# Reordering the slot of a Mamba-2 layer with routed experts: B and C first, the next sequence's first chunk before the additions, and a mean square summed in four column groups

## The chip, the cores and the metric

The kernel runs on one core of a Trainium2 chip. The metric is the device time of one execution in microseconds (us), the median of several runs; lower is better. The profile comes from one further execution.

## What is computed

Sixteen sequences of 512 tokens of width 128 go through two layers. The first is a Mamba-2 block: an input projection gives z (256 wide), x (256), B (128), C (128) and one step size for each of 4 heads; x, B and C pass a causal convolution of 4 taps and a SiLU; then a state-space scan runs over the tokens; its result y is normalised, gated and projected back. The second is a mixture of 8 experts of which each token takes 2.

```python
xBC = silu(conv(x @ Win.T) + conv_b)          # x_ssm, B, C
h   = dA_t * h + (dt_t * x_t) B_t             # for each token, head by head
y_t = C_t . h + D * x_t
yn  = y * rsqrt(mean(y * y) + eps) * norm_w   # the mean square of the change
out = (yn * silu(z)) @ Wout.T
x   = layernorm(x + out)
x   = layernorm(x + experts(x))               # top 2 of 8
```

## The kernel before, in words

Each engine has its program written out by hand; semaphores join them. Phase one is a row of slots. In slot s the scan of sequence s runs in four chunks of 128 tokens (c = 0 to 3), while sequence q = s + 1 is projected and convolved and sequence r = s - 1 (and s - 2) is routed, that is its rows are written to DRAM sorted by expert. A preparatory slot (`enter_all`) precedes slot 0; slots 1 to 14 have the same content, slot 15 projects nothing. Phase two takes the sorted rows through the experts, tile by tile, from about 402 us on; the change doesn't touch it.

The scan of a chunk, by engine:

- TensorE (`slot_pe`): `exponents` (L527: six bf16 matmuls, the logarithms of the decays for 4 heads, into bank `pl[c % 2]`), transposes of the chunk's x and B (L715 to L723), the matmul of C with the carried state (L727), one block of the next sequence's projection (`project_block`, L512), the masked products with x (L750, weights of 64 columns), the carried part (L756), and the new state (L767).
- ScalarE (`slot_act`): `exp_exponents` (L847), copies of B and of the first state (L1016, L1010), tap 0 of the convolution (`tap0`, L911), the squares of y (`square`, L976).
- VectorE (`slot_dve`): `mask_chunk` (L1222: decays times the products of B and C, `Gm`), the x scaled by its step (`Xdt`, L1429), `carried` (L1435), taps 1 to 3 (L1141), y (L1449), state (L1455).
- GpSimd (`slot_pool`): the x scaled for the state (`decay_x`, L1709), the decayed state (`decay_state`, L1703), the gate (`gate_y`, L1659), the places of the routed rows (`place_rows`) and eight indirect DMA writes (`scatter`, L1696), strictly in the order written.

Between the last chunk of slot s and the first of slot s + 1 lies the border. TensorE: `z_block(q, 0)` (L520), the column sums of the squares (L781: for each chunk two matmuls with the squares as weights and 96 columns of ones moving), four output blocks (L802), in between the transposes of the next x (`turn_first_x`, L594), then `inner_products` (L658: B times C of the next sequence, into bank p7) and `z_block(q, 1)`. ScalarE: four SiLUs of the convolution in the order x, x, B, C (`activate`, L917), two products with the skip weight (L922), the gate's two SiLUs (L933) with the copy of the products (`keep_products`, L928) between them. VectorE: the last taps, the gates' top two, the mean square from p7 (L1484), the picks, the four additions of the residual (`residual`, L1247), and in the next slot the first mask and the first scaled x. GpSimd: scatters and the power -1/2 (L1762).

ScalarE holds one table of functions at a time; Exp and SiLU lie in different ones, so an `ACT_TABLE_LOAD` stands in its stream where a chunk's first Exp follows the SiLUs, and one where the SiLUs follow. TensorE's projection into bank `pj[0]` for the next slot waits until ScalarE has read z out of that bank:

```python
if k == 0:
    wait(pe, sz_ready, CC * (q.n - 1) + 1)
```

Of the kernel before, what the change touches and what calls it, by code (L numbers as in the profile page):

```python
# [33 lines left out]
XC = CC + 2  # L34
TAPS = 4
# [20 lines left out]
SP_STEPS = 13  # L56
SP_AHEAD = 9
# [35 lines left out]
def build(nc, t, out):  # L93
    ctx = ExitStack()
    with ctx:
# [78 lines left out]
        gt = sb("gt", [P, CC, TOKS])  # L174
        ms = sb("ms", [P, NC])
# [97 lines left out]
        def y_bank(j):  # L273
# [28 lines left out]
                     "sp_step", "a_ready", "tap_done", "conv_done", "carried_ready", "ln_step", "ve_ready", "shift_ready",  # L302
                     "u_ready", "gate_step", "chosen_ready", "ms_ready", "pos_step", "rank_read",
                     "rows_ready", "parts_ready", "split_step")
        (x1_ready, Gm_ready, M_ready, Xdt_ready, v_ready, yv_ready, state_ready, sp_step, a_ready,
         tap_done, conv_done, carried_ready, ln_step, ve_ready, shift_ready, u_ready, gate_step, chosen_ready,
         ms_ready, pos_step, rank_read, rows_ready, parts_ready, split_step) = [sem(n) for n in names_dve]
        names_pool = ("slot_ready", "place_step", "picks_made", "Xdd_ready", "decayed_ready", "g_ready", "rms_ready", "rstd_ready", "scaled_ready")
        (slot_ready, place_step, picks_made, Xdd_ready, decayed_ready, g_ready, rms_ready, rstd_ready, scaled_ready) = [sem(n) for n in names_pool]
        scattered = [[sem(f"scattered_{'AB'[k]}{i}") for k in range(2)] for i in range(2)]  # L310
        table_step = sem("table_step")
# [55 lines left out]
        def out_place(c):  # L367

            return (p5, c * OUTW) if c + 1 < NC else (p4, 0)
# [136 lines left out]
        def _(pe):  # L506
            def project_block(q, k):
                if k == 0:
                    wait(pe, sz_ready, CC * (q.n - 1) + 1)
                else:  # L510
                    wait(pe, conv_done, XC * q.n + k - 1)
                pe.matmul(pj[k % 2][:, :], w_xbc[:, k * P:(k + 1) * P], xT[:, q.n, :],  # L512
                          start=True, stop=True).then_inc(proj_psum, 1)
# [92 lines left out]
            def enter_all():  # L606
# [38 lines left out]
                steps_of(3)  # L645
                turn_steps(3)
# [5 lines left out]
            def inner_products(q):  # L652

                pe.wait_ge(xc_ready, XC * (q.n + 1))
# [42 lines left out]
            def slot_pe(s, scan, project, route):  # L697
# [4 lines left out]
                for c in range(NC):  # L702
                    tok = slice(c * P, (c + 1) * P)
                    n = NC * s.n + c
                    if scan and c != 1 and (c + 1 < NC or project):
                        if not route and c == 0:
                            pe.wait_ge(steps_kept, SEQS // GROUP)
                        exponents(s if c + 1 < NC else q, (c + 1) % NC)
                    if scan:
                        pe.wait_ge(Xdt_ready, n) if not isinstance(n, int) or n > 0 else None  # L710
                        wait(pe, Btok_ready, (NC - 1) * s.n + c)
                        if c == 0:
                            wait(pe, x1_ready, NC * s.n)
                        if c == 0:
# [14 lines left out]
                    if project:  # L729
# [46 lines left out]
                if scan:  # L776
                    pe.wait_ge(sq_done, NC * (s.n + 1))
                    pe.wait_ge(yv_ready, NC * (s.n + 1))
                    for c in range(NC):
                        for k in range(CC):  # L780
                            mm = pe.matmul(p7[:, c * PADN:(c + 1) * PADN], ysq[:, k, c * P:(c + 1) * P],  # L781
                                           ones[:, 0:PADN], start=(k == 0), stop=(k == CC - 1))
                    mm.then_inc(ss_psum, 1)
                if scan:
# [4 lines left out]
                    for c in range(NC):  # L789
                        if c + 1 == NC:  # L790
# [4 lines left out]
                            elif project:  # L795
                                pe.wait_ge(S_ready, q.n + 1)
                                turn_first_x(q)
# [7 lines left out]
                if project:  # L805
                    inner_products(q)
# [29 lines left out]
        def _(act):  # L836
# [71 lines left out]
            def tap0(q, c):  # L908
                act.wait_ge(proj_psum, XC * q.n + c + 1)
                wait(act, xc_ready, XC * (q.n - 1) + c + 1)  # L910
                act.activation(acc[:, c, :], pj[c % 2][:, :], ACT.Identity, bias=conv_b[:, c:c + 1],  # L911
                               scale=conv_w[:, c, TAPS - 1:TAPS]).then_inc(tap0_done, 1)

            def activate(q, k):
                act.wait_ge(conv_done, XC * q.n + k + 1)
                wait(act, y_psum, NC * (q.n - 1))
                act.activation(xc[q.par][:, k, :], acc[:, k, :], ACT.Silu).then_inc(xc_ready, 1)  # L917

            def skip_part(q, k):
                act.wait_ge(xc_ready, XC * q.n + k + 1)  # L920
# [14 lines left out]
            def enter_all():  # L935
# [26 lines left out]
                keep_steps(3)  # L962
                enter_dt(1, G0, SEQS)
# [887 lines left out]
```

## Time and profile before

| | |
|---|---|
| runs | 701.42, 702.55 and 702.74 us, median 702.55 us |
| profiled execution | 699.86 us, its span on the core 698.0 us |
| TensorE clock granted, mean | 0.977 |
| busy share of the span | TensorE 91%, VectorE 78%, ScalarE 69%, GpSimd 67% |
| one slot in the steady part | 22.5 us |

A row of a timeline gives the start of an instruction (or of several alike), its length, engine, line, operation and tiles, and in brackets how long the engine had been idle and who ended that. Lengths of two neighbours can overlap: an engine starts the next instruction before the last one's result is out. So what an instruction costs its engine is the distance of two starts, and what it costs a waiter is its length. A float32 matmul shows as two records.

### The profile page before, as it was taken

Reading aid. Unit: us, or ns where it says so; the run is one execution under the profiler, and the core shown is the slowest. Engines: PE = TensorE matmul, PEld = TensorE weight load, DVE = VectorE, ACT = ScalarE, POOL = GpSimd, SP = SyncE. Lnnn points to the kernel's source line nnn. Section 1 sums busy time; section 2 is a strip of 40 time slices with the busy share of each in tenths; the row PEclk is TensorE's granted clock in tenths of the full one; section 3 lists DMA queues with packets and bytes.
Section 4 is the critical chain, followed back from the end, with each engine's and each line's share of the span. In section 5 each row is a group of like instructions: output and inputs, shape, how many; then the busy total and the mean of one; then the engine's idle time right before and its main releaser. Section 6 shows DMA issues by size and latency. Waiting matters only on the chain.

```text
span 698.0 us, 19510 instructions
## 1 busy us (share of the span) xinstructions
PE 633.0 (91%) x4811; PEld 507.4 (73%) x4811; DVE 542.1 (78%) x1852; ACT 479.5 (69%) x1210; POOL 466.9 (67%) x696
## 2 busy tenths in 40 slices
PE   6789999999999999999998789999999999999900
PEld 4356666666566766666665589999999999999900
DVE  4688898899988998889989577776666666888844
ACT  5567877887787878887786377556665566677724
POOL 5023287788777887788777857777755555777754
PEclk9999999999999999999999999999999999999965
DMA  9280001110111011110110123323422223455352
GB/s 248 56 301 17 13 24 35 39 48 24 38 36 45 29 38 32 44 47 25 35 36 32 43 60 88 92 76 110 98 75 71 74 73 101 137 183 176 122 201 100
DMA packets 56668, 54.50 MB, mean 78 GB/s; under 512 B 9562, under 2 KB 45918, under 8 KB 56304
## 3 DMA queue, kind: packets, MB, share of 16 engines
q1 hardware_dynamic: 45840, 33.67, 17.5%
q0 software_dynamic: 8416, 16.93, 7.1%
q10 hardware_dynamic: 2304, 2.65, 1.1%
q8 instruction: 44, 0.72, 0.5%
q14 instruction: 64, 0.52, 0.3%
HBM read 31.05 MB, written 22.63 MB: 77 GB/s over the span
## 4 chain that ended last, share of the span: by engine, by line
PE 62%; issue 11%; POOL 9%; ACT 6%; DVE 5%; DMA 4%; SPq 1%; DVEq 1%; POOLq 0%; ACTq 0%
PE p L693 12%; PE pl L684 8%; PE pj L512 5%; PE p L684 4%; PE p L756 3%; PE p L727 3%; PE p L781 3%; PE p L750 3%; POOL moe_rows L1772 3%; PE p L802 3%; PE p L767 3%; PE pj L520 2%; PE p L658 2%; PE pj L676 1%; PE pl L533 1%
## 5 line engine op out<-in xcount | busy, mean ns | idle before, releaser
L1772 POOL DMA_INDIRECT moe_rows<-xT x135 | 135.5, 1004 | 78.9 <-DVE xT L1389 49.0
L1696 POOL DMA_INDIRECT sorted_rows<-pair,slot x128 | 128.6, 1005 | 30.6 <-issue 28.4
L1141 DVE SCALAR_TENSOR_TENSOR acc<-pj,conv_w_sb,acc 128x511 f32<-128x511 f32 (+2 forms) x192 | 141.0, 735 | 8.6 <-ACT acc L911 6.8
L693 PE MATMUL p<-w,xT 128*128 x1080 | 143.7, 276 | 2.2 <-ACT xT L1058 1.7
L1058 ACT ACTIVATE xT<-pl,b_sb 128x128 f32<-128x128 f32 x360 | 102.7, 368 | 48.7 <-PE pl L684 46.2
L693 PEld LDWEIGHTS p<-w,xT 128*128 128x128 f32 x1080 | 131.4, 192 | 3.5 <-issue 3.4
L684 PE MATMUL pl<-xT 128*128 128x128 f32 x720 | 95.1, 275 | 1.6 <-DVE xT L1377 1.6
L684 PEld LDWEIGHTS pl<-xT 128*128 128x128 f32 x720 | 87.5, 192 | 1.8 <-issue 1.8
L1385 DVE TENSOR_TENSOR xT<-p,b_sb 128x128 f32<-128x128 f32 x135 | 39.2, 290 | 63.1 <-PE p L693 58.3
L1058 ACT ACTIVATE xT<-p,b_sb 128x128 f32<-128x128 f32 x180 | 51.4, 370 | 23.9 <-PE p L684 23.7
L512 PE MATMUL pj<-xT,w_xbc 128*128 128x512 f32 x128 | 67.2, 607 | 0.0
L911 ACT ACTIVATE acc<-pj,conv_b_sb,conv_w_sb 128x512 f32<-128x512 f32 x64 | 49.7, 777 | 22.2 <-PE pj L512 21.3
L1709 POOL TENSOR_TENSOR Xdd<-Xdt,cur 128x256 f32<-128x256 f32 x48 | 29.5, 615 | 45.3 <-DVE Xdt L1429 32.0
L1377 DVE COPY xT<-w 128x512 f32 x135 | 58.7, 435 | 0.0
L750 PEld LDWEIGHTS p<-M,Xdt 128*64 128x64 f32 x512 | 26.8, 136 | 43.7 <-issue 42.9
L1659 POOL TENSOR_TENSOR gt<-yv,sz 128x256 f32<-128x256 f32 x64 | 47.1, 735 | 9.5 <-DVE yv L1449 8.8
L1389 DVE SCALAR_TENSOR_TENSOR xT<-xT 128x128 f32<-128x128 f32 x135 | 49.4, 366 | 4.8
L1222 DVE TENSOR_TENSOR M<-pl,Gm 128x512 f32<-128x512 f32 x64 | 43.9, 686 | 11.4 <-issue 8.5
L847 ACT ACTIVATE pl<-pl 128x512 f32<-128x512 f32 x64 | 37.2, 582 | 20.8 <-PE pl L538 20.6
L684 PE MATMUL p<-xT 128*128 128x128 f32 x360 | 47.6, 275 | 0.0
L750 PE MATMUL p<-M,Xdt 128*64 128x128 f32 x512 | 42.1, 285 | 2.0 <-issue 1.2
L684 PEld LDWEIGHTS p<-xT 128*128 128x128 f32 x360 | 43.7, 192 | 0.0
(235 smaller groups left out, 1340.2 us busy)
## 6 DMA issues: line engine op xcount, KB each, us to landing
xT<-sorted_rows SPq DMA_DIRECT2D x135, 65.0 KB
xres<-in_x SPq DMA_DIRECT2D x16, 256.0 KB, 3.1
w<-in_w SPq DMA_DIRECT2D x2, 2048.0 KB, 10.0
acc<-moe_rows SPq DMA_DIRECT2D x12, 256.0 KB, 3.8
xT<-moe_rows SPq DMA_DIRECT2D x12, 256.0 KB, 5.4
out<-sz ACTq DMA_DIRECT2D x10, 256.0 KB, 2.4
moe_rows<-xT POOLq DMA_INDIRECT x135, 2.3
sorted_rows<-pair,slot POOLq DMA_INDIRECT x128
```

Of the source, the lines that this page charges most:

```text
L512: pe.matmul(pj[k % 2][:, :], w_xbc[:, k * P:(k + 1) * P], xT[:, q.n, :], start=True, stop=True).then_inc(proj_psum, 1)
L684: mm = pe.matmul(h_bank[j % 3][:, f * P:(f + 1) * P], w1e[j % 4][:, f * P:(f + 1) * P], sT[j % 4], start=True, stop=True)
L693: mm = pe.matmul(y_bank(j)[:, 0:P], hT[j % 4][:, f, :], w2[:, bass.ds(e, 1), f, :].rearrange("p e d -> p (e d)"), start=(f == 0), stop=(f ...
L750: mm = pe.matmul(p7[half, (h // 2) * P:(h // 2 + 1) * P], Xdt[c % 2][:, h * HD:(h + 1) * HD], M[c % 2][:, h, :], start=(h < 2), stop=(c == ...
L911: act.activation(acc[:, c, :], pj[c % 2][:, :], ACT.Identity, bias=conv_b[:, c:c + 1], scale=conv_w[:, c, TAPS - 1:TAPS]).then_inc(tap0_do ...
L1058: act.activation(hT[j % 4][:, f, :], h_bank[j % 3][:, f * P:(f + 1) * P], ACT.Gelu, bias=b1[:, bass.ds(e * FB + f, 1)]).then_inc(hT_ready, 1)
L1141: ins = dve.scalar_tensor_tensor(out=acc[:, k, j:TOKS], in0=pj[k % 2][:, 0:TOKS - j], scalar=conv_w[:, k, TAPS - 1 - j:TAPS - j], in1=acc[ ...
L1377: dve.tensor_copy(w1e[j % 4], w1[:, bass.ds(expert[j], 1), :].rearrange("p e f -> p (e f)")).then_inc(w1e_ready, 1)
L1389: dve.scalar_tensor_tensor(out=ye[j % 8], in0=ye[j % 8], scalar=xs[k][:, P + 1:P + 2], in1=xs[k][:, 0:P], op0=ALU.mult, op1=ALU.add).then_ ...
L1659: pool.tensor_tensor(gt[:, :, c * P:(c + 1) * P], yv[c % 2][:, :, :], sz[s.par][:, :, c * P:(c + 1) * P], ALU.mult).then_inc(g_ready, 1)
L1696: pool.indirect_dma_start(out=sorted_rows[:, :], out_offset=bass.IndirectOffsetOnAxis(slot[q.par][:, c, k:k + 1], 0), in_=(rowA, rowB)[k][ ...
L1772: pool.indirect_dma_start(out=moe_rows[:, :], out_offset=bass.IndirectOffsetOnAxis(xs[k][:, P:P + 1].bitcast(I32), 0), in_=ye[j % 8], in_o ...
```

## The change

1. The blocks of the projection are taken in the order B, C, x, x (`ORDER`), so B and C are convolved and activated first.
2. `inner_products` needs only B and C and moves between the second and the third output block; `turn_first_x` goes right behind it. ScalarE copies the products before the skip products, and both gate SiLUs come last.
3. From slot 1 on, `mask_chunk(q, 0)` and the scaled x of the next sequence's chunk 0 come before `residual` on VectorE, and its `decay_x` comes ahead of the last scatter on GpSimd.
4. `exponents` of chunk 1 of the next sequence are computed in chunk 3 of this slot, together with those of chunk 0, and both are exponentiated there. At the border no Exp is left; the first one of a slot is that of chunk 2. In the preparatory slot the same is done for sequence 0.
5. `project_block(q, 0)` goes ahead of the transpose of B.
6. The mean square: the ones become the weights (32 columns), the squares move, and chunk c writes partitions 32c to 32c + 31 (its own group of columns of the array). ScalarE copies the 128 x 128 sums (`keep_sums`, behind the first SiLU), TensorE transposes them after the first output block, VectorE reads the mean square from there.

```diff
+ORDER = (*range(CC, XC), *range(CC))
...
         def out_place(c):
-            return (p5, c * OUTW) if c + 1 < NC else (p4, 0)
+            return (p5, (c - 1) * OUTW) if c > 0 else (p4, 0)
...
             def turn_first_x(q):
-                pe.wait_ge(xc_ready, XC * q.n + CC)
+                pe.wait_ge(xc_ready, XC * (q.n + 1))
...
             def inner_products(q):
-                pe.wait_ge(xc_ready, XC * (q.n + 1))
+                pe.wait_ge(xc_ready, XC * q.n + XC - CC)
...
             # enter_all, TensorE
                 steps_of(3)
+                pe.wait_ge(steps_kept, SEQS // GROUP)
+                exponents(q, 1)
                 turn_steps(3)
...
             # slot_pe
-                    if scan and c != 1 and (c + 1 < NC or project):
-                        if not route and c == 0:
-                            pe.wait_ge(steps_kept, SEQS // GROUP)
-                        exponents(s if c + 1 < NC else q, (c + 1) % NC)
+                    if scan and c == 2:
+                        exponents(s, 3)
+                    if project and scan and c == 3:
+                        exponents(q, 0)
+                        exponents(q, 1)
...
                         if c == 0:
+                            if project:
+                                project_block(q, 0)
                             wait(pe, x1_ready, NC * s.n)
...
-                    for c in range(NC):
-                        for k in range(CC):
-                            mm = pe.matmul(p7[:, c * PADN:(c + 1) * PADN], ysq[:, k, c * P:(c + 1) * P],
-                                           ones[:, 0:PADN], start=(k == 0), stop=(k == CC - 1))
+                    for k in range(CC):
+                        for c in range(NC):
+                            mm = pe.matmul(p7[Q * c:Q * (c + 1), 0:P], ones[:, 0:Q], ysq[:, k, c * P:(c + 1) * P],
+                                           start=(k == 0), stop=(k == CC - 1), skip_group_check=True)
...
+                        if c == 1:
+                            pe.wait_ge(sums_kept, s.n + 1)
+                            pe.transpose(p7[:, P:2 * P], kept[:, :], ident[:, :]).then_inc(turned_psum, 1)
+                        if c == 2 and project:
+                            inner_products(q)
+                            if route:
+                                turn_first_x(q)
...
             # slot_act
-                    if scan and (c + 1 < NC or project):
+                    if scan and 0 < c < NC - 1:
                         exp_exponents(n + 1, c + 1)
+                    if scan and project and c == NC - 1:
+                        exp_exponents(n + 1, 0)
...
                     if scan and c > 0:
                         square(s, c - 1)
+                    if scan and project and c == NC - 1:
+                        exp_exponents(n + 2, 1)
...
                     for k in range(XC):
                         activate(q, k)
+                        if k == 0:
+                            keep_sums(s)
+                    keep_products(q)
                     for k in range(CC):
                         skip_part(q, k)
-                    gate_part(q, 0)
-                    keep_products(q)
-                    gate_part(q, 1)
+                    for k in range(CC):
+                        gate_part(q, k)
...
             # slot_dve
-                    dve.wait_ge(ss_psum, s.n + 1)
+                    dve.wait_ge(turned_psum, s.n + 1)
...
+                if project and s.n > 0:
+                    dve.wait_ge(cur_ready, q.n + 1)
+                    mask_chunk(q, 0)
+                    scale_x(q, 0)
                 if scan:
                     residual(s)
...
             # slot_pool
-                    for c in range(2, NC):
-                        scatter(old, c, 1)
+                    scatter(old, 2, 1)
+                if project and s.n > 0:
+                    pool.wait_ge(cur_ready, q.n + 1)
+                    decay_x(q, 0)
+                if scatters:
+                    scatter(old, 3, 1)
```

## Rows read from the trace of the kernel before

**Rows 1.** The page: busy time by engine, and the last chain by engine.

```profile
PE 633.0 (91%) x4811; PEld 507.4 (73%) x4811; DVE 542.1 (78%) x1852; ACT 479.5 (69%) x1210; POOL 466.9 (67%) x696
...
PE 62%; issue 11%; POOL 9%; ACT 6%; DVE 5%; DMA 4%; SPq 1%; DVEq 1%; POOLq 0%; ACTq 0%
```

**Rows 2.** Busy time by window: PE, PEld, DVE, ACT, POOL, granted clock, DMA, GB/s.

```profile
200.00:250.00 50.00, 48.55 (x336) 32.23 (x334) 44.92 (x147) 38.72 (x81) 39.93 (x68) 1.00 0.12 35
```

**Rows 3.** Timeline of ScalarE, one border and the next.

```profile
191.92 0.42 ACT L976 ACTIVATE ysq<-yv 128x256 f32<-128x256 f32 x1 [0.33 <-DVE yv L1449]
192.35 1.28 ACT L917 ACT_TABLE_LOAD   x1
193.65 2.19 ACT L917 ACTIVATE xc<-acc 128x512 f32<-128x512 f32 x4
195.75 1.32 ACT L922 ACTIVATE xD<-xc,skip 128x512 f32<-128x512 f32 x2
196.97 0.57 ACT L933 ACTIVATE sz<-pj 128x512 f32<-128x512 f32 x1
...
198.92 1.28 ACT L847 ACT_TABLE_LOAD   x1
...
200.71 0.27 ACT L1016 COPY Btok<-p 128x128 f32<-128x128 f32 x1
200.87 0.79 ACT L911 ACTIVATE acc<-pj,conv_b_sb,conv_w_sb 128x512 f32<-128x512 f32 x1
...
202.40 0.38 ACT L1010 COPY state<-p 128x256 f32<-128x256 f32 x1
...
214.87 1.28 ACT L917 ACT_TABLE_LOAD   x1
```

**Rows 4.** Timeline of TensorE, the same stretch.

```profile
192.39 2.02 PE L781 MATMUL p<-ones,ysq 128*128 128x96 f32 x16
194.25 1.58 PE L802 MATMUL p<-w_out,gt 128*128 128x136 f32 x12
...
196.35 1.05 PE L658 MATMUL p<-xc 128*128 128x128 f32 x8
197.25 1.02 PE L520 MATMUL p<-xT,w_z 128*128 128x512 f32 x2
...
201.04 0.39 PE L533 MATMUL pl<-too_early,ident_b 128*128 128x512 bf16 x1 [0.34 <-ACT Btok L1016]
...
209.60 0.67 PE L767 MATMUL p<-Xdd,Btok 128*128 128x256 f32 x2
210.11 0.38 PE L533 MATMUL pl<-too_early,ident_b 128*128 128x512 bf16 x1
...
210.76 0.39 PE L721 MATMUL p<-ident,xc 128*128 128x128 f32 x2
211.15 0.70 PE L727 MATMUL p<-state,xc 128*128 128x256 f32 x2
211.69 1.02 PE L512 MATMUL pj<-xT,w_xbc 128*128 128x512 f32 x2
```

**Rows 5.** Timeline of GpSimd, the same stretch.

```profile
193.30 0.75 POOL L1659 TENSOR_TENSOR gt<-yv,sz 128x256 f32<-128x256 f32 x1
...
202.85 0.61 POOL L1703 TENSOR_TENSOR decayed<-state,cur 128x256 f32<-128x256 f32 x1 [0.58 <-ACT state L1010]
...
215.80 0.74 POOL L1659 TENSOR_TENSOR gt<-yv,sz 128x256 f32<-128x256 f32 x1
```

**Rows 6.** Timeline of TensorE and ScalarE at the first slot's border.

```profile
39.21 0.63 PE L538 MATMUL pl<-S,pick_t 96*128 96x128 bf16 x4
...
39.51 1.28 ACT L847 ACT_TABLE_LOAD   x1
```

**Rows 7.** Timeline of ScalarE, first Gelu of phase two.

```profile
405.15 1.28 ACT L1058 ACT_TABLE_LOAD   x1 [8.18 <-PE pl L684]
```

**Rows 8.** Timeline of TensorE, 32-column weights in four groups.

```profile
29.77 1.07 PE L557 MATMUL pl<-xT,w_dt 128*32 128x512 f32 x8
```

More of the change, by code:

```diff
@@ L56 @@
 SP_STEPS = 13
+DT_STEPS = SP_STEPS + 3
 SP_AHEAD = 9
@@ L174, in build @@
         gt = sb("gt", [P, CC, TOKS])
+        kept = sb("kept", [P, P])
         ms = sb("ms", [P, NC])
@@ L310, in build @@
         scattered = [[sem(f"scattered_{'AB'[k]}{i}") for k in range(2)] for i in range(2)]
+        sums_kept = sem("sums_kept")
+        turned_psum = sem("turned_psum")
         table_step = sem("table_step")
@@ L511, in project_block @@
                     wait(pe, conv_done, XC * q.n + k - 1)
-                pe.matmul(pj[k % 2][:, :], w_xbc[:, k * P:(k + 1) * P], xT[:, q.n, :],
+                pe.matmul(pj[k % 2][:, :], w_xbc[:, ORDER[k] * P:(ORDER[k] + 1) * P], xT[:, q.n, :],
                           start=True, stop=True).then_inc(proj_psum, 1)
@@ L728, in slot_pe @@
                                       start=True, stop=True).then_inc(off_psum, 1)
-                    if project:
+                    if project and c > 0:
                         project_block(q, c)
@@ L789, in slot_pe @@
                     for c in range(NC):
-                        if c + 1 == NC:
+                        if c == 0:
                             if not route:
@@ L916, in activate @@
                 wait(act, y_psum, NC * (q.n - 1))
[L917 removed]
+                act.activation(xc[q.par][:, ORDER[k], :], acc[:, k, :], ACT.Silu).then_inc(xc_ready, 1)
             def skip_part(q, k):
[L920 removed]
+                act.wait_ge(xc_ready, XC * q.n + XC - CC + k + 1)
                 wait(act, yv_ready, NC * (q.n - 1))
@@ L962, in enter_all @@
                 keep_steps(3)
+                exp_exponents(1, 1)
                 enter_dt(1, G0, SEQS)
@@ L977, in square, with keep_sums @@
                                ACT.Square).then_inc(sq_done, 1)
+            def keep_sums(s):
+                act.wait_ge(ss_psum, s.n + 1)
+                wait(act, turned_psum, s.n)
+                act.copy(kept[:, :], p7[:, 0:P]).then_inc(sums_kept, 1)
             def normalise(r, k):
@@ L1040, in slot_act @@
                     decay(2, G0, SEQS, 2, 4)
+                if scan and not project:
+                    keep_sums(s)
                 if project:
@@ L1043, in slot_act @@
                         activate(q, k)
+                        if k == 0:
+                            keep_sums(s)
+                    keep_products(q)
                     for k in range(CC):
                         skip_part(q, k)
-                    gate_part(q, 0)
-                    keep_products(q)
-                    gate_part(q, 1)
+                    for k in range(CC):
+                        gate_part(q, k)
             slots(act, slot_act)
@@ L1173, in softplus_step @@
                 else:
-                    dve.wait_ge(sp_step, SP_STEPS * g + k)
+                    dve.wait_ge(dt_step, DT_STEPS * g + k)
                 if k == 0:
@@ L1207, in split @@
                 high, mid, low = (parts[:, lo:hi, Q * k:Q * k + NH] for k in range(3))
-                link = chain(split_step, 3 * g)
+                link = chain(dt_step, DT_STEPS * g + SP_STEPS)
                 dve.wait_ge(sums_psum, g + 1)
@@ L1224, in mask_chunk, with scale_x @@
                                   ALU.mult).then_inc(M_ready, 1)
+            def scale_x(s, c):
+                dve.wait_ge(tr_psum, NC * s.n + c + 1)
+                wait(dve, Xdd_ready, (NC - 1) * s.n + max(c - 1, 0))
+                o, at = x0_bank(s.n) if c == 0 else (p5, 0)
+                dve.tensor_tensor(heads(Xdt[c % 2][:, :]), heads(o[:, at:at + DI]),
+                                  per_head(cur[s.par][:, 0, :], c), ALU.mult).then_inc(Xdt_ready, 1)
             def take_ranks(r):
@@ L1416, in slot_dve @@
                     return
-                if scan:
+                if scan and s.n < 2:
                     dve.wait_ge(cur_ready, s.n + 1)
@@ L1420, in slot_dve @@
                 for c in range(NC):
-                    n = NC * s.n + c
                     if project and c > 0:
                         tap(q, c - 1, 1)
-                    if scan:
-                        dve.wait_ge(tr_psum, n + 1)
-                        wait(dve, Xdd_ready, (NC - 1) * s.n + max(c - 1, 0))
-                        o, at = x0_bank(s.n) if c == 0 else (p5, 0)
-                        dve.tensor_tensor(heads(Xdt[c % 2][:, :]), heads(o[:, at:at + DI]),
-                                          per_head(cur[s.par][:, 0, :], c), ALU.mult).then_inc(Xdt_ready, 1)
+                    if scan and (c > 0 or s.n < 2):
+                        scale_x(s, c)
+                    n = NC * s.n + c
                     if route and c == 0:
@@ L1728, in slot_pool @@
                     return
-                if scan:
+                if scan and s.n < 2:
                     pool.wait_ge(cur_ready, s.n + 1)
```

21 lines of the change are left out of this document (9 added, 12 removed).

## The prediction

> **What bounds the kernel now.** I read the page first: TensorE is busy 91% of the span and carries 62% of the chain that ended last [rows 1]. In 50 us of steady slots it is busy 48.55, VectorE 44.92, ScalarE 38.72, GpSimd 39.93, at full clock [rows 2]. That looks like a kernel bound by TensorE, in which each microsecond saved there counts. A busy share doesn't say that, so I read the timelines of one slot next, and the reader is to see a handing-over in them.
>
> Take as zero the load of the SiLU table at 192.35; the next one is at 214.87, so a slot is 22.52 us [rows 3]. It has two stretches.
>
> *Stretch A, from the SiLU table to the copy of the first state* (192.35 to 202.40 + 0.38 = 202.78): 10.43 us. ScalarE is nearly always at work in it: a table load of 1.30, four SiLUs in 2.10, two skip products in 1.22, gate and products, a second load and the Exp of chunk 1 (198.92 to 200.71, 1.79), the copy of B, tap 0, the Exp of chunk 2, the state. TensorE in the meantime works ahead, then waits for the copy of B (0.34 idle at 201.04) [rows 3, 4].
>
> *Stretch B, from that copy to the next SiLU table*: 12.09 us. Here TensorE goes through chunks 1 to 3 with hardly a gap. GpSimd runs beside it without rest: it begins 0.07 after the copy (202.85) and ends the last gate at 215.80 + 0.74 = 216.54, 13.76 us after the copy [rows 5]. The output blocks need that gate. At the border before, it ended at 193.30 + 0.75 = 194.05, and the output blocks began at 194.25 [rows 4, 5], straight behind the column sums. So TensorE and GpSimd arrive together: a shorter column sum finds the gate not ready.
>
> **The change part by part.** I cost each against these two stretches.
>
> *Column sums.* Eight matmuls take 192.39 to 194.25, 1.86 us [rows 4]. The new form resembles the step sizes' matmul, where four of 512 columns in four groups end after 1.07 [rows 8], while a single one of 512 columns over the full array has a length of 1.02 [rows 4]: the four run side by side. Two rounds at 128 columns should then take some 0.6 (estimate: two quarters of 0.86 and a little for the switch); the upper bound is 1.86, if nothing overlaps. The Trainium skill says the same in "TensorEngine Tiling (Array Packing)", Tiling Modes: up to 4 times faster with 32 columns, but a change of mode drains the array. By its factor alone the sums would take 0.47; the drain is not seen apart in a row here. Saved: about 1.25 of TensorE. Worth on the path: at most the 0.20 between the gate's end and 194.25, and that is eaten by the next item.
>
> *Copy and transpose of the sums.* New: a 128 x 128 copy on ScalarE behind the first SiLU. There is no such row; the copy of B has its shape and holds ScalarE 0.16 (200.71 to 200.87), with its result out after 0.27 [rows 3]. Bounds 0.16 and 0.27. It lies on stretch A, as ScalarE is its bound: +0.16. TensorE stands still for it behind the first output block.
>
> *Border, laid out anew from the load of the SiLU table.* Load 1.30, one SiLU to 1.83, the copy to 1.99 (result 2.10), three more to 3.57. TensorE turns the sums (0.11), ends the second output block at about 2.7 (0.47 each, as three take 1.42 up to 195.67, my estimate from the twelve records), the products take 0.90 (196.35 to 197.25) and their result is out at 3.8. ScalarE so waits 0.23, copies the products (0.48, as the gate's SiLU of the same shape), skip products 1.22 to 5.50, first gate SiLU out at 6.07. Only then may the next projection begin: result 1.02 later, and the transpose of B, now behind it, about 0.15 more: 7.24. Copy of B 0.16, tap 0 0.67, **table load 1.30**, Exp 0.49, state 0.38, with signals: 10.3. Before: 10.43. Gain 0.15 a slot. An Exp has gone from the border, but its table load hasn't: it now stands behind tap 0 and before the Exp of chunk 2, still on the path. Where it stands against that Exp's wait matters. At slot 0's border the load began at 39.51, while the matmuls the Exp waits for ran to 39.84 [rows 6]: it starts ahead of the wait.
>
> *Mask, scaled x, decay_x ahead.* Nothing is added. VectorE gets the products at 4.4, ends mask and scaled x at 5.35 and the four additions at about 6.5; these gate the transpose of B, which is at 7.0 anyway. The cover is the projection in front of it; without that, the 0.9 of the two would show. On GpSimd `decay_x` waits for the scaled x, 5.4, with one scatter queued behind it; both are over by 7.4, and the next thing there needs the statistics at about 8.1. Cost nothing.
>
> *Exponents of chunk 1 moved into chunk 3.* TensorE: six bf16 matmuls, 210.11 to 210.76, 0.65 [rows 4]. Before, they stood at the border, where TensorE has slack; now they stand in stretch B, where it has none. Part is taken back: between 210.76 and 211.15 two transposes and a wait for the state take 0.39, of which I put 0.17 down to the wait, and the restart costs 0.10 (211.15 to 211.69 for 0.44 of work, an estimate). So +0.38. ScalarE gets the Exp (0.49) between two squares; the gap before the last square was 0.33 [rows 3], and it shifts with the rest, so up to +0.05. If rather the whole 0.65 is hidden by the state coming later through VectorE, this is 0; if nothing is taken back, 0.65.
>
> Sum: -0.15 + 0.43 = +0.28 a slot. Laid out with a uniform 0.04 for each signal, where the state's wait is longer, I get +0.08. I take **+0.2**, for 14 steady slots +2.8. Slot 1 has its first x turned behind the projection now, +0.5; the preparatory slot and slot 0 about nothing (turning the steps waits for the new exponents, 0.6, but the products come sooner); slot 15, which projects nothing, starts its scan sooner, -0.5. Phase two is untouched and shifts. Together +2.8, say +3. Against the profiled execution, 699.86 us (span 698.0, 1.9 around it), that is 702.8; against the median of the runs, 2.7 higher, 705.5. I forecast the median.
>
> **The rivals.** What a measurement of this kernel can tell from no change is about 0.2%, 1.4 us.
>
> *Faster: the moved exponents are free.* If stretch B doesn't grow, the slot keeps the 0.15, and up to 0.3 if the border's queue is tighter than laid out: 14 times that, -2 to -4, 699 to 700. In its strong form TensorE itself is the bound, as the chain's 62% says: 1.25 - 0.11 saved 16 times gives -18, 684. Against the strong form: TensorE waits for ScalarE and the gate [rows 4, 5]. It decides from the point where stretch B grows by less than 0.15.
>
> *About the same:* the two stretches cancel, 701 to 704.
>
> *Slower by more: the table load stands behind the wait.* The first Gelu's load began only after 8.18 us of idle time, when its matmul was out [rows 7]. If the Exp of chunk 2 does so, its load starts at 8.7 and not 8.1 in stretch A: +0.55 a slot, 713. The page "ScalarE: Activation LUTs", Step-by-step, of the Trainium skill puts the load right before its ACTIVATE; whether a wait stands between is not said, and [rows 6] speaks for no delay.
>
> *Slower: the groups don't overlap.* Then the sums' copy comes 0.3 later and pushes all SiLUs: +0.3, 709.5.
>
> **How the numbers follow.** Forecast (slower by 1.4 to 6): 0.38. Faster 0.32, of it 0.05 for the strong form. Same 0.20. Table load 0.05, groups 0.05. The predicted time is the likeliest one's, 705.5. The range takes the weak faster form with a margin and the groups' case: 697 to 711, leaving out the strong form, most of the table case and the tails. The likeliest case alone: 704 to 708.5. Faster 0.32, same 0.20, slower 0.48.
>
> **What would show it.** Slot length 22.7 (between two SiLU table loads). Column sums about 0.6, followed by an idle TensorE of some 0.9 until the gate, and another until the copy of the sums. First state copied 10.3 after the SiLU table; TensorE idle about 1.0 ahead of the matmul with the state (L727) in chunk 1. The two exponents side by side in chunk 3, 1.3 long. Tables still 2 a slot. I am wrong if the slot is under 22.4, above all if the border (SiLU table to first state) is under 10 us or stretch B stays at 12.1; or if the residual holds up the transpose of B.

## The result and the profile after

The changed kernel takes 719.95 us (median of 4 runs, 719.07 to 720.29) beside 701.98 us for the kernel before (4 runs, 699.22 to 702.74): ratio 1.0257, 95% interval 1.0228 to 1.0287. The profiled execution took 719.07 us, its span is 717.2 us, 19.2 more than before.

The page, and the busy times of 50 us of steady slots (the lines that answer to [rows 1, 2]):

```profile
PE 625.3 (87%) x4827; PEld 492.5 (69%) x4827; DVE 545.7 (76%) x1852; ACT 479.6 (67%) x1226; POOL 466.0 (65%) x696
...
PE 60%; issue 12%; ACT 11%; POOL 8%; DVE 4%; DMA 2%; DVEq 1%; SPq 1%; ACTq 0%; POOLq 0%
...
L517 PE MATMUL pj<-xT,w_xbc 128*128 128x512 f32 x128 | 68.6, 618 | 8.9 <-ACT sz L947 8.9
```

```profile
200.00:250.00 50.00, 45.52 (x332) 28.55 (x330) 44.14 (x137) 38.16 (x81) 39.12 (x65) 1.00 0.11 36
```

TensorE did 7.7 us less work and the kernel takes 19 us longer. ScalarE's share of the chain has gone from 6% to 11%, and the projection waits for the gate's SiLU, which is new. The slots, each from one SiLU table load to the next, say where the time is (us):

| | before | after | difference |
|---|---|---|---|
| start to the first SiLU load | 33.34 | 33.74 | +0.40 |
| slot 0 | 23.73 | 24.93 | +1.20 |
| slot 1 | 22.52 | 27.00 | +4.48 |
| slot 2 | 22.52 | 23.66 | +1.14 |
| slots 3 to 14 | 12 x 22.55 | 12 x 23.36 | +9.7 |
| last border and slot 15, to the Gelu load | 32.44 | 36.14 | +3.70 |
| phase two | 292.85 | 291.43 | -1.42 |

**A steady slot.** ScalarE's timeline, answering to [rows 3]:

```profile
202.76 1.28 ACT L931 ACT_TABLE_LOAD   x1
204.05 0.63 ACT L931 ACTIVATE xc<-acc 128x512 f32<-128x512 f32 x1
204.59 0.25 ACT L997 COPY kept<-p 128x128 f32<-128x128 f32 x1
204.74 1.67 ACT L931 ACTIVATE xc<-acc 128x512 f32<-128x512 f32 x3
206.73 0.58 ACT L942 COPY Gm<-p 128x512 f32<-128x512 f32 x1 [0.33 <-PE p L665]
207.21 1.33 ACT L936 ACTIVATE xD<-xc,skip 128x512 f32<-128x512 f32 x2
208.45 0.58 ACT L947 ACTIVATE sz<-pj 128x512 f32<-128x512 f32 x1
208.93 0.59 ACT L947 ACTIVATE sz<-p 128x512 f32<-128x512 f32 x1
210.47 0.27 ACT L1038 COPY Btok<-p 128x128 f32<-128x128 f32 x1 [0.95 <-issue]
210.63 0.78 ACT L925 ACTIVATE acc<-pj,conv_b_sb,conv_w_sb 128x512 f32<-128x512 f32 x1
211.43 1.28 ACT L861 ACT_TABLE_LOAD   x1
212.72 0.58 ACT L861 ACTIVATE pl<-pl 128x512 f32<-128x512 f32 x1
213.22 0.38 ACT L1032 COPY state<-p 128x256 f32<-128x256 f32 x1
...
226.12 1.28 ACT L931 ACT_TABLE_LOAD   x1
```

Stretch A, from the load at 202.76 to the end of the state's copy at 213.60, is 10.84 (before 10.43); stretch B is 12.52 (before 12.09). ScalarE now idles twice in A, 0.33 for the products and 0.95 for the transposed B, and the second table load starts only after the second gap. TensorE, answering to [rows 4]:

```profile
202.79 0.65 PE L790 MATMUL p<-ysq,ones 128*32 128x128 f32 x16
204.05 0.73 PE L817 MATMUL p<-w_out,gt 128*128 128x136 f32 x4 [0.61 <-POOL gt L1694]
...
205.57 1.13 PE L665 MATMUL p<-xc 128*128 128x128 f32 x8
...
209.18 1.10 PE L517 MATMUL pj<-xT,w_xbc 128*128 128x512 f32 x2 [0.48 <-ACT sz L947]
210.11 0.27 PE L724 MATMUL p<-ident,xc 128*128 128x128 f32 x1
...
211.48 0.38 PE L543 MATMUL pl<-S,pick_t 96*128 96x128 bf16 x4
...
213.65 0.70 PE L736 MATMUL p<-state,xc 128*128 128x256 f32 x2 [0.97 <-ACT state L1032]
```

The column sums are 0.65 long where they were 2.02. TensorE then waits for GpSimd's last gate (0.61), for the gate's SiLU (0.48) and for the state (0.97).

**The borders that aren't steady.** TensorE's timeline in slot 0, at the border from slot 0 to slot 1, at the last border and in the last slot, and ScalarE's load for the first Gelu:

```profile
39.79 2.08 PE L517 MATMUL pj<-xT,w_xbc 128*128 128x512 f32 x2 [1.97 <-ACT sz L947]
...
58.73 0.64 PE L790 MATMUL p<-ysq,ones 128*32 128x128 f32 x16
61.47 0.98 PE L607 MATMUL p<-vals,ones 128*128 128x192 f32 x2 [2.09 <-DVE parts L1242]
62.24 1.11 PE L817 MATMUL p<-w_out,gt 128*128 128x136 f32 x4
...
394.50 1.13 PE L665 MATMUL p<-xc 128*128 128x128 f32 x8 [1.94 <-DVE ms L1515]
...
395.68 1.83 PE L817 MATMUL p<-w_out,gt 128*128 128x136 f32 x8
...
414.37 0.65 PE L790 MATMUL p<-ysq,ones 128*32 128x128 f32 x16 [0.96 <-ACT ysq L991]
417.28 1.28 PE L817 MATMUL p<-w_out,gt 128*128 128x136 f32 x4 [2.27 <-POOL gt L1694]
418.35 0.42 PE L810 MATMUL p<-ident,kept 128*128 128x128 f32 x1
418.56 2.93 PE L817 MATMUL p<-w_out,gt 128*128 128x136 f32 x12
...
425.77 1.28 ACT L1086 ACT_TABLE_LOAD   x1 [10.43 <-PE pl L691]
```

In the kernel before, the last output blocks were:

```profile
399.93 2.12 PE L802 MATMUL p<-w_out,gt 128*128 128x136 f32 x16 [0.88 <-POOL gt L1659]
```

At 61.47 the sums of the second group of sequences (`sums(G0, SEQS, (ones,), 3)`) wait for a split on VectorE. They share bank p4 with one output block. `out_place` used to give p4 to block 3, now it gives it to block 0, so the wait stands ahead of all four blocks. After the gaps of 2.09 and 2.27 the matmuls take up to twice as long: four records of an output block 1.11 where they take 0.63 at full speed, and in the last slot the twelve records of three blocks 2.93 where they lasted 1.58 [rows 4]. The granted clock of 417 to 426 us is 0.50, the lower of its two levels (1.2 and 2.4 GHz) throughout; that of 60 to 82 us is 0.92, before it was 1.00. At 394.50 the products wait for a mean square that VectorE delivers behind the early part of the routing table. There the eight records of the products are still near full speed, 1.13, and the blocks behind them are not, 1.83 for eight records.

### The profile page after: what moved, and what is told of

Same layout as the page of the kernel before. It is cut to its first block, busy times and chain, and to the rows that moved or that the text cites. A ratio compares the mean times of both kernels' runs of the same rounds, so it can differ in the third digit from the quotient of the medians.

```text
span 717.2 us, 19559 instructions
## 1 busy us (share of the span) xinstructions
PE 625.3 (87%) x4827; PEld 492.5 (69%) x4827; DVE 545.7 (76%) x1852; ACT 479.6 (67%) x1226; POOL 466.0 (65%) x696
## 4 chain that ended last, share of the span: by engine, by line
PE 60%; issue 12%; ACT 11%; POOL 8%; DVE 4%; DMA 2%; DVEq 1%; SPq 1%; ACTq 0%; POOLq 0%
PE p L700 12%; PE pl L691 8%; PE pj L517 8%; PE p L691 4%; PE p L759 4%; POOL moe_rows L1811 3%; PE p L736 3%; PE p L776 3%; PE p L765 3%; ACT xD L936 3%; PE p L665 2%; PE pl L538 2%; PE pl L543 2%; PE pl L540 2%; ACT pl L861 2%
## 5 line engine op out<-in xcount | busy, mean ns | idle before, releaser
L1694 POOL TENSOR_TENSOR gt<-yv,sz 128x256 f32<-128x256 f32 x64 | 47.0, 734 | 10.5 <-DVE yv L1480 9.8
L1250 DVE TENSOR_TENSOR M<-pl,Gm 128x512 f32<-128x512 f32 x64 | 43.8, 684 | 10.5 <-ACT Gm L942 10.2
L817 PE MATMUL p<-w_out,gt 128*128 128x136 f32 x256 | 42.6, 304 | 10.0 <-POOL gt L1694 10.0
L817 PEld LDWEIGHTS p<-w_out,gt 128*128 128x128 f32 x256 | 37.1, 210 | 14.0 <-POOL gt L1694 13.8
```

What stands on the lines that cost most here:

```text
L817: mm = pe.matmul(o[:, at:at + OUTW], gt[:, k, c * P:(c + 1) * P], w_out[:, k, :], start=(k == 0), stop=(k == CC - 1), skip_group_check=True)
```

## The experiments

The kernel before took about 702 us on some devices and about 742 on others. There is no trace of it from the slower ones. Run 1's trace is from one of them: its steady slots are 22.52 as here, and its phase two takes 335.9 where the kernel before took 292.85. So totals are given as ratios to the kernel before on the same device, and slots are compared directly. "Last stretch" is from the last SiLU load to the Gelu load (32.44 in the kernel before).

**1. The column groups alone** (`sums_alone`: the kernel before with part 6).

> The kernel before with part 6 alone (mean square in four column groups, its copy and transpose). Theory of the border: TensorE's saved 1.2 us a slot is not on the path, because the last gate on GpSimd ends only 0.2 us before the output blocks began; the copy of the sums (0.15 on ScalarE) and the wait of the mean square's readers add a little. Slot 22.5 to 22.8, total 702 to 707. Rival 'TensorE is the bound': slot 21.4, total 685. Rival 'the sums' chain is what costs': slot 23.0 or more, total 709 or more.

Ratio 1.0047 (1.0021 to 1.0073). That is inside what was expected. The steady slot stayed 22.52, as TensorE idles 0.96 where it saved 1.2:

```profile
195.04 0.64 PE L785 MATMUL p<-ysq,ones 128*32 128x128 f32 x16
196.65 0.73 PE L809 MATMUL p<-w_out,gt 128*128 128x136 f32 x4 [0.96 <-POOL gt L1675]
...
400.10 0.64 PE L785 MATMUL p<-ysq,ones 128*32 128x128 f32 x16 [0.97 <-DVE yv L1465]
403.01 1.28 PE L809 MATMUL p<-w_out,gt 128*128 128x136 f32 x4 [2.27 <-POOL gt L1675]
...
404.29 2.93 PE L809 MATMUL p<-w_out,gt 128*128 128x136 f32 x12
```

The last stretch grew from 32.44 to 35.59. Before, the longer column sums filled part of the time until the gate and TensorE idled 0.88 there; now it idles 2.27 and comes back at half speed. From the start of these output blocks to the Gelu load it is 8.50 (403.01 to 411.51), before 5.22 (399.93 to 405.15): a saving that is only waited out costs 3.3 in this slot. Slot 0 was 1.0 longer as well.

**2. The exponents alone** (`exps_alone`: the kernel before with part 4).

> The kernel before with part 4 alone (exponents and Exp of the next sequence's chunk 1 in chunk 3, none at the border). Theory: the stretch from the first state's copy to the SiLU table grows by 0.4 as in the changed kernel; the stretch before it loses the Exp (0.49), since in the old order nothing else waits at the border. Slot 22.4 to 22.6, total 700 to 704. Rival 'moving the exponents is the whole loss': slot 22.9 or more, total 708 or more. The load of the Exp table then stands behind tap 0.

Ratio 1.0039 (1.0019 to 1.0059). Slot 22.74: stretch A fell from 10.43 to 9.95, stretch B rose from 12.09 to 12.79. The slot is above the 22.4 to 22.6 that were expected: the move does shorten the border, and the scan gives back more than that.

**3. The changed kernel without part 4** (`exps_back`).

> The changed kernel without part 4: exponents and Exp of chunk 1 back at the border. Theory: the stretch behind the first state's copy falls from 12.52 to 12.1; in the stretch before it the table load moves into the 0.95 us in which ScalarE waited for the transpose of B, so it does not grow although an Exp of 0.49 comes back: 10.84 to 10.3. Slot 22.3 to 22.5, total 704 to 707. Rival 'the border's new order costs, wherever the exponents are': only the 0.4 comes back, slot 22.9 to 23.0, total 713 to 714.

Ratio 1.0137 (1.0108 to 1.0167), steady slot 22.85: A 10.77, B 12.08. Stretch B is the old one again, so its 0.43 belongs to the exponents alone. Stretch A keeps most of its loss, as the rival had it: that loss comes from the orders. At the border of slot 1 this version has the same wait of 2.09 as the changed kernel, but TensorE comes out of it at full speed:

```profile
60.83 0.56 PE L607 MATMUL p<-vals,ones 128*128 128x192 f32 x2 [2.09 <-DVE parts L1240]
61.23 0.63 PE L818 MATMUL p<-w_out,gt 128*128 128x136 f32 x4
```

Its slot 1 takes 24.52, in the changed kernel 27.00.

**4. Output block 0 of sequence 0 in its old place** (`slot0_placed`).

```diff
-        def out_place(c):
+        def out_place(s, c):
+            if s.n == 0:
+                return (p5, c * OUTW) if c + 1 < NC else (p4, 0)
...
-                        if c == 0:
-                            if not route:
+                        if not route and c + 1 == NC:
                                 sums(G0, SEQS, (ones,), 3)
```

> The changed kernel with the output blocks of sequence 0 placed as before (block 3 in bank p4), so that the sums over the late sequences wait for VectorE only ahead of the last block and not ahead of the first. Theory: TensorE's idle 2.1 us and the half clock behind it go; the time from the SiLU table of slot 1's start to the next (27.0 against 22.5 before) falls to about 23.7; total 3 to 4 us less than the changed kernel, 716 to 717. Rival 'VectorE's softplus and the late first x do it': under 1 us less. The steady slot stays at 23.36.

Slot 1 fell from 27.00 to 24.11 and the wait of 2.09 is gone: the place of block 0 is the main cause of slot 1. The ratio, 1.0278 (1.0230 to 1.0325), doesn't show it: the steady slots were 23.52 in this profile, and the last stretch 37.50, both longer than in the changed kernel. In the last stretch the products behind the wait for the mean square ran at half speed here, 2.05 for 1.13. Why stretch B was 12.68 in the steady slots, not 12.52, is not known; the changed kernel was not run on that device.

**5. The changed kernel again** (`after_again`), as the companion of 6 to 8.

> The changed kernel once more, beside the next three, since the last four ran where all kernels take some 40 us longer in phase two. Slower than before by 16 to 20 us, steady slot 23.3 to 23.5.

721.32 us, ratio 1.0262 (1.0223 to 1.0301), slot 23.38.

**6. The first gate's SiLU ahead of the products' copy** (`gate_early`).

```diff
+                    gate_part(q, 0)
                     keep_products(q)
                     for k in range(CC):
                         skip_part(q, k)
-                    for k in range(CC):
-                        gate_part(q, k)
+                    gate_part(q, 1)
```

> The changed kernel with the first gate SiLU (z out of bank pj0) ahead of the products' copy and the skip products on ScalarE. Theory: the next projection no longer waits for ScalarE (0.48 idle before it) but follows z directly; the transpose of B, tap 0, the table load and the first state come 0.5 to 0.6 sooner; slot 23.36 to 22.8, total 7 to 8 us less than the changed kernel. Rival 'the table load and GpSimd set the time': under 0.2 a slot.

716.64 us, ratio 1.0192 (1.0153 to 1.0231). Slot 22.90: A 10.38, B 12.52. The SiLU fills the wait for the products and the projection starts behind z without a gap. The direction was right. The gain, 0.47 a slot and 4.7 in all, is less than the 7 to 8 expected: TensorE now does z, projection and transpose without a gap, and its own work is what ends last. Phase two was also 2.4 longer in this profile than in run 5's.

**7. The table loaded in the gap** (`table_early`: an Exp on 128 x 4 numbers behind the gate's SiLUs).

```diff
+                    act.activation(touched[:, :], neg_half[:, :], ACT.Exp)
```

> The changed kernel with an Exp on 128 x 4 constants (result unused) behind the gate's SiLUs, so that the Exp table is loaded while ScalarE waits for the transpose of B, and not behind tap 0. Theory: the load leaves the path, the copy of B and tap 0 come 0.55 later, the first state 0.7 sooner; slot 23.36 to 22.6 or 22.7, total 9 to 11 us less than the changed kernel. Rival 'the projection's wait is what counts': under 0.2 a slot, or slower.

714.73 us, ratio 1.0173 (1.0133 to 1.0212). Slot 22.76: A 10.23, B 12.53. ScalarE's timeline:

```profile
205.89 0.59 ACT L948 ACTIVATE sz<-p 128x512 f32<-128x512 f32 x1
206.50 1.28 ACT L1078 ACT_TABLE_LOAD   x1
207.80 0.21 ACT L1078 ACTIVATE touched<-neg_half 128x4 f32<-128x4 f32 x1
207.91 0.25 ACT L1039 COPY Btok<-p 128x128 f32<-128x128 f32 x1
```

The load of 1.28 falls into the 0.95 of idleness and comes off the chain behind tap 0. It gives 0.61 a slot, as expected. The total fell by 6.6 and not by 9 to 11: the last stretch was 37.24 (35.76 in run 5), with its products at half speed as in run 4.

**8. The mean square as before** (`sums_back`: the changed kernel without part 6).

> The changed kernel with the mean square as before (96 columns of ones moving, read from p7 without copy and transpose). Theory: in the steady slot the sums' 1.2 us more fill TensorE's wait for the gate and for the copy, ScalarE saves 0.15: slot within 0.15 of 23.36. In the last slot TensorE no longer idles 2.3 us before its output blocks and keeps its full clock there: the time from the last SiLU table to the Gelu table falls by 3. Total 3 to 5 us less than the changed kernel. Rival 'the four groups save on the path': slot 0.5 or more longer, total 4 or more us longer.

717.38 us, ratio 1.0198 (1.0149 to 1.0246). The steady slot is 23.36, as with the groups, and A 10.81: the 0.15 of the kept copy only shortens the wait for the products. The gain sits in slot 1 (27.05 to 25.29; the gap is 0.91 and the clock stays up) and in the last stretch (35.76 to 33.97). Two rows of TensorE from that stretch:

```profile
393.52 2.04 PE L665 MATMUL p<-xc 128*128 128x128 f32 x8 [1.86 <-DVE ms L1508]
...
417.37 2.12 PE L814 MATMUL p<-w_out,gt 128*128 128x136 f32 x16 [0.90 <-POOL gt L1687]
```

From the start of the last output blocks to the Gelu load it is 5.24 again, as in the kernel before; the changed kernel has 8.49. The 1.5 that remain arise at the border before: the same wait for the mean square as in the changed kernel, 1.86, but here the products behind it run at half speed.

**9. Only the orders** (`order_only`: parts 4 and 6 and `out_place` of sequence 0 undone, gate early as in 6, the products of the fifteenth slot's border behind the last output block).

> The changed kernel with four things undone and one order turned: chunk 1's exponents back at the start of the next slot (part 4), the column sums as before (part 6), output block 0 of sequence 0 in its old place, the inner products of the fifteenth slot behind the last output block as before; and the first gate's SiLU ahead of the products' copy. What is left of the change is B and C first, products, mask and scaled x ahead of the additions. Theory 'the orders are sound but for what stood with them': the steady slot was 22.85 with the exponents back, its stretch A 10.77 with a wait of 0.45 for the products and 0.15 of kept copy in it; both go, so A 10.2 to 10.3, B 12.1, slot 22.3 to 22.4, slot 0 to 1 near 23, last slot near 32.4: 696 to 701. Rival 'B and C first costs of itself, since the first x and the products come no sooner and VectorE's taps are in the way': slot 22.6 to 22.9, time 703 to 708.

706.97 us (12 runs), ratio 1.0058 (1.0041 to 1.0075). Slot 22.52, A 10.42, B 12.10: to the hundredth the slot of the kernel before. Once the waits are out, B and C first brings nothing and costs nothing in a steady slot. The first expectation missed in both numbers, the rival in the slot; its time fits, for other reasons. The time above the kernel before is in the start and slot 0 (+2.6 together), slot 1 (+0.7) and the last stretch (36.07). There my own edit was bad: the first x was left between the output blocks, TensorE waited 2.42 for it and ran at half speed through the products.

**10. The same with part 4 and the early table** (`all_but_exponents_undone`).

> The same, but with chunk 1's exponents moved as in the changed kernel, and a tiny Exp behind the gate's SiLUs, so that its table is loaded while TensorE projects. Theory 'orders sound, moved exponents cost stretch B what they cost in it': A 10.1 or less, B 12.5, slot 22.5 to 22.7, time 701 to 706. Rival 'with all waits out of stretch A the exponents' 0.67 of TensorE come off it': A 9.6 to 9.8, slot 22.1 to 22.3, time 696 to 700.

708.89 us (6 runs), ratio 1.0089 (1.0062 to 1.0117). Slot 22.68: A 10.01, B 12.67. The slot came as the first theory had it, with B 0.17 above it; the time missed by 3. Against 9 the exponents' move and the early table together gain 0.41 in A, and B costs 0.57 more.

**11. More work in the last slot** (`last_thrice`).

```diff
+                    for again in range(1 if project else 3):
                         for k in range(CC):
```

> The changed kernel, but in the last slot alone the column sums in four groups are done three times over (32 matmuls more, same result), which fills 1.3 us of the 2.27 us in which TensorE had nothing to do ahead of the last output blocks. Theory 'the gap halves the clock': output blocks at 0.65 a group of eight or less than 2.2 for sixteen instead of 2.93 for twelve, first expert's matmuls 1.1 instead of 2.05, last slot 1.5 to 3 shorter, time 717 to 718.5 beside 720 to 721. Rival 'the 32-column matmuls themselves bring the clock down': still 2.93 and 2.05, last slot unchanged or longer.

TensorE's timeline:

```profile
416.96 1.52 PE L791 MATMUL p<-ysq,ones 128*32 128x128 f32 x48 [0.97 <-ACT ysq L992]
419.88 0.73 PE L818 MATMUL p<-w_out,gt 128*128 128x136 f32 x4 [1.40 <-POOL gt L1695]
...
420.55 1.55 PE L818 MATMUL p<-w_out,gt 128*128 128x136 f32 x12
...
425.56 1.39 PE L691 MATMUL pl<-xT 128*128 128x128 f32 x8 [3.23 <-DVE xT L1414]
```

With three times the 32-column matmuls and a gap of 1.40 in place of 2.28 the same twelve records last 1.55, at full speed (granted clock 1.00). So the 32-column matmuls don't slow the clock, the idleness behind them does. The time didn't follow: 721.08 us beside 721.32 on another device, ratio 1.0263 beside 1.0262. VectorE's copy of the first expert's rows follows its mean square by 4.0 as in the changed kernel, so TensorE, done sooner, waits 3.23 for it (2.45 in run 5), and behind that gap the granted clock is 0.61. The last stretch is 1.27 shorter, but the part up to slot 1 was 1.4 longer in this profile. The expectation of the time is a miss.

**12. Another way to shorten stretch A** (`state_early`: the kernel before and nothing of the change).

```diff
                         if c + 1 < NC:
+                            if c == 0:
+                                exponents(s, 2)
                             pe.wait_ge(Btok_ready, (NC - 1) * s.n + c + 1)
                             pe.wait_ge(Xdd_ready, (NC - 1) * s.n + c + 1)
                             if c == 0:
-                                exponents(s, 2)
...
-                    if scan and (c + 1 < NC or project):
-                        exp_exponents(n + 1, c + 1)
                     if scan and c == 1:
...
                         act.copy(state[0][:, :], p6[:, DI:2 * DI]).then_inc(state_ready, 1)
+                    if scan and (c + 1 < NC or project):
+                        exp_exponents(n + 1, c + 1)
```

> The kernel before with none of the change. Two orders are turned in the stretch from the SiLU table load to the state copy, which every version so far shows to be set by a chain: B token-major, chunk 2's exponents, the state's outer product, the state copy. Chunk 2's exponents stand ahead of the wait for B token-major (TensorE idles 0.34 there), and ScalarE copies the state ahead of chunk 2's Exp (0.50). Theory 'that chain sets the stretch': the state copy ends 0.3 to 0.4 sooner, L727 likewise, and nothing in the second stretch waits for chunk 2's Exp before 203.9: slot 22.1 to 22.3, time 697 to 700. Rival 'ScalarE's sum sets the slot': the Exp is only moved and the slot stays 22.5, time 702. Rival 'the Exp falls on the path to chunk 2's mask': slot 22.6 to 22.9, time 704 to 707.

740.09 us beside 741.32 (12 and 17 runs), ratio 0.9986 (0.9972 to 0.9999): the only version faster than the kernel before, and just: the interval ends at 0.9999. The state was out 9.99 after the SiLU load, 0.44 sooner, more than expected. The slot is 22.43, between the theory and the first rival: B grew from 12.09 to 12.44. TensorE and GpSimd in chunk 2, where TensorE had run through at 209.60 [rows 4]:

```profile
208.91 0.67 PE L768 MATMUL p<-Xdd,Btok 128*128 128x256 f32 x2 [0.35 <-POOL Xdd L1710]
```

```profile
207.03 1.08 POOL L1697 DMA_INDIRECT sorted_rows<-pair,slot  x1 [0.21 <-issue]
208.14 0.63 POOL L1710 TENSOR_TENSOR Xdd<-Xdt,cur 128x256 f32<-128x256 f32 x1
```

GpSimd's scatter stands ahead of the scaled x, in the order written, and holds GpSimd for 1.08. TensorE, 0.4 sooner, waits 0.35 there, and B grew by as much, 0.35.

## Why the prediction was wrong

The steady slots of all versions on one scale:

| | A | B | slot |
|---|---|---|---|
| before | 10.43 | 12.09 | 22.52 |
| predicted for the change | 10.3 | 12.5 | 22.7 |
| changed | 10.84 | 12.52 | 23.36 |
| changed, without exponents moved (3) | 10.77 | 12.08 | 22.85 |
| changed, gate early (6) | 10.38 | 12.52 | 22.90 |
| changed, table early (7) | 10.23 | 12.53 | 22.76 |
| orders only (9) | 10.42 | 12.10 | 22.52 |
| orders and exponents (10) | 10.01 | 12.67 | 22.68 |
| before, exponents alone (2) | 9.95 | 12.79 | 22.74 |
| before, state early (12) | 9.99 | 12.44 | 22.43 |

**Right: stretch B.** The exponents of chunk 1 in chunk 3 were priced at 0.43, measured 0.43 in the changed kernel. The terms hold too. TensorE's last carried part, before and after:

```profile
213.23 0.71 PE L756 MATMUL p<-ident,carried 128*128 128x128 f32 x4
```

```profile
224.41 0.71 PE L765 MATMUL p<-ident,carried 128*128 128x128 f32 x4
```

It starts 10.45 behind the first state's copy before and 10.81 after, 0.36 for the 0.38 put on TensorE; the way from there to the SiLU table grew by 0.07, for the 0.05 put on ScalarE. The rival "the moved exponents are free" fell with runs 2, 3 and 10.

**Right: the column sums are hidden.** Priced at 0.6, measured 0.65, and worth nothing in a steady slot (runs 1 and 8). TensorE's idle time until the gate was 0.61, not 0.9. The strong form of the faster rival, TensorE as the bound, and the rival "the groups don't overlap" are refuted. The mask, the scaled x and the residual held up nothing: the transpose of B came straight behind the projection.

**Right: the table load doesn't wait for its Exp's matmuls.** It began at 211.43, the matmuls of that Exp ran to 211.86 (211.48 + 0.38).

**Wrong by its size: the border's layout, "Gain 0.15 a slot".** It was a loss of 0.41. I had laid out the chain by starts and a rough signal, and nearly every link was a bit short (times from the SiLU table load). The gate's SiLU was out at 6.27 where I had 6.07: the products came 0.14 later than laid out. B was transposed at 7.62 where I had 7.24: besides the 0.20 of the SiLU, 0.15 passed from its end to the projection, for which I had put nothing. The load came 0.80 behind the start of tap 0, not 0.67, since it didn't overlap the instruction ahead of it. That makes 0.51 of the 0.54 between 10.30 and 10.84. With a gain of 0.15 left over from a sum of 10.3, errors of 5% decided the sign.

**Wrong in kind, behind that size.** In the kernel before ScalarE was the only long chain of the stretch. Its second table load (198.92 to 200.20 [rows 3]) ran beside TensorE's projection:

```profile
198.88 1.02 PE L512 MATMUL pj<-xT,w_xbc 128*128 128x512 f32 x2
```

The change made one chain through two engines: four SiLUs with the products between them, skip products, gate's SiLU, projection, transpose of B, its copy, tap 0, and only then the load. I saw that the load was "still on the path", and didn't ask what ScalarE would do instead while TensorE projects: nothing, for 0.95. Runs 6 and 7 take the chain apart at two places and get 0.46 and 0.61 back in A.

**Missed: "slot 0 about nothing" and "slot 1 +0.5".** In slot 0 stretch A took 11.65, before 10.47. That border has no output blocks, so TensorE had nothing to do until the gate's SiLU: it idled 1.97 and the projection behind took 2.08 (39.79), before 1.71 without a wait. For slot 1, the diff shows `out_place` turned round, and I didn't follow what else is tied to block 0. It cost 4.5: a wait of 2.1, half the clock behind it, and the products late by as much. Run 4 gets 2.9 of it back, run 8 1.8. Run 3, with the same wait and the clock up, is 2.5 shorter, 0.5 of it the shorter steady slot; so some 2.0 are the clock (an estimate from these slots).

**Missed: "slot 15, -0.5".** It was +3.7. Of that, 3.3 lies behind the column sums' gap, where the clock is down: from the start of the last output blocks to the Gelu load 8.49 for 5.22 (run 1 alone has 8.50, run 8 5.24, run 11 7.19). I had treated it as a saving waited out. The other 0.4 is the border before it, where the products wait for VectorE's mean square; where the clock falls at those products, as in runs 4, 7 and 8, this border costs more, 1.5 in run 8. I had costed the move of the products by the steady slot, where the mean square comes in time.

The sum, 19.2 where I had 3: slots 3 to 14 gave 7.3 more than forecast, the start and the other slots 10.5 more (slot 1 3.8, the last stretch 4.2, slots 0 and 2 and the start 2.5), phase two 1.4 less. Open is what in the start and slot 0 (1.6 longer in the profile shown, up to 4.4 in the others) belongs to the change and what is spread between executions, why the clock falls behind a wait in one profile and not in another, and 0.3 of the 1.14 of slot 2, which the versions with the exponents moved show in its stretch B.

## What to carry to other kernels

Ask of each engine in a border what it does while the other works on what it is waiting for. A step with a fixed cost and no input, such as a table load, belongs in that gap, and a tiny operation puts it there. Cost a reordering at the first, second and last round of a loop too: the waits that stand there once are tied to a place, and moving the place moves the wait ahead of work that had been in front of it. And where two stretches are held by different engines, an early end of one may be taken by the other: run 12 kept 0.1 of 0.44, while runs 6 and 7, which only took back what the change had added, kept all of their 0.46 and 0.61.

## What the runs showed of the hardware

- In the last slot TensorE, after 0.65 us of column sums and a gap of 2.27, comes back at half speed, matmuls 2.93 for 1.58 and granted clock 0.50; after 1.52 and a gap of 1.40 (run 11), or 2.02 and 0.90 (run 8), it doesn't. So a shorter piece of work ahead of an unchanged wait can cost more than it saves. The length of the gap doesn't decide it alone: after 2.09 in slot 1, four records took 1.11 in the changed kernel and 0.63 in run 3.
- Eight matmuls with 32-column weights in four groups, 128 columns moving, are 0.65 long; eight over the whole array with 96 columns moving were 2.02.
- The table load for the Exp starts right behind the preceding instruction's end, 0.05 before the last matmuls that the Exp waits for begin, but it doesn't overlap that preceding instruction: 0.80 from tap 0's start, where a copy behind another tap 0 starts after 0.67 (223.93 to 224.60). The first Gelu's load does not run ahead in this way: it came after 10.43 of idleness, when the matmul was out (before, 8.18 [rows 7]).
- Devices differ in phase two, not in the slots: from the Gelu load to the end 335.9 us in run 1 and 332.2 in run 12, 292.85 in the profile before, and run 1's steady slot is 22.52 like that one's.
